# One exponential per pair of heads over two adjacent PSUM banks, and waits per K-chunk for the first output tile of three projections, in an eight-core hybrid (state space, attention, gated FFN) kernel

## The reference, cut to what matters

```python
g = y * silu(z)
g = g * rsqrt(mean(g ** 2) + EPS) * norm_w
x = x + einsum('bld,df->blf', g, out_proj_w)      # state-space layer, its end
...
r = sigmoid(xr @ W_r.T);  k = xk @ W_k.T          # FFN
x = x + r * (square(relu(k)) @ W_v.T)
...
att = einsum('bhqd,bhkd->bhqk', q, k) * (1.0 / sqrt(D))      # attention, 16 heads
att = softmax(where(causal, att, -inf), axis=-1)
x = x + einsum('bhqk,bhkd->bhqd', att, v) @ w_proj + b_proj
```

## Time and profile before

| | |
|---|---|
| median of 2 runs | 9809.84 us (9798.19 to 9821.5) |
| the profiled execution | 9709.57 us |
| its span, slowest core (5) | 9708.0 us (all cores 9662.8 to 9708.0) |
| TensorE matmuls, weight loads | 5080.3 us (52%), 2045.3 us (21%) |
| VectorE | 3306.1 us (34%) |
| ScalarE | 2614.5 us (27%) |
| mean granted clock of TensorE, core 5 | 0.694 |
| attention, all blocks, with what lies between them | about 5990 to 8700 us of the span |

### The profile page before, as it was taken

How to read it: one execution, slowest core, us unless ns; L and a number is a source line. 1 busy time by engine, 2 the same in 40 slices (tenths; PEclk the granted TensorE clock), 3 DMA queues, 4 the chain that set the end, 5 groups by cost and what they waited for, 6 DMA issues and landing times.

```text
span 9708.0 us, 88191 instructions; the slowest of 8 cores (9662.8 to 9708.0 us)
## 1 busy us (share of the span) xinstructions
PE 5080.3 (52%) x21232; PEld 2045.3 (21%) x21232; DVE 3306.1 (34%) x6508; ACT 2614.5 (27%) x4592; POOL 148.4 (2%) x234
## 2 busy tenths in 40 slices
PE   0235645646546552555245665566666666653555
PEld 0223223223223230221011221111111111111222
DVE  0444454454444443455323233221110101013444
ACT  0113123122232130000101112355557575741111
POOL 2000000000000000000100000000000000000000
PEclk9556756757657665777567776567778787876776
DMA  6330101101101102000332221100000000002001
GB/s 102 94 102 26 60 9 51 60 1 60 50 10 60 36 24 44 35 35 35 75 82 74 77 65 58 35 28 31 31 19 13 31 1 31 1 18 52 35 37 42
DMA packets 336322, 420.16 MB, mean 43 GB/s; under 512 B 120993, under 2 KB 181026, under 8 KB 335778
## 3 DMA queue, kind: packets, MB, share of 16 engines
q1 hardware_dynamic: 247314, 360.00, 11.8%
q0 software_dynamic: 88528, 54.52, 3.6%
HBM read 331.39 MB, written 119.87 MB: 46 GB/s over the span
## 4 chain that ended last, share of the span: by engine, by line
PE 36%; DVE 23%; ACT 16%; DMA 11%; issue 11%; DVEq 1%; SPq 1%; POOL 1%; ACTq 1%; POOLq 0%
ACT pt_sb L191 10%; PE pB L191 9%; PE pA L191 7%; PE pE L191 6%; PE pD L191 5%; PE pF L191 4%; PE pC L191 4%; ACT D L191 3%; DVE y L191 2%; DVE t1b L191 2%; DMA wtmp<-win_l 2%; DVEq L189 1%; DMA xtm<-x 1%; ACT tr L191 1%; DMA wq_sb<-wqkv_l 1%
## 5 line engine op out<-in xcount | busy, mean ns | idle before, releaser
L191 DVE TENSOR_TENSOR pt_sb<-pt_sb,mask01b 128x128 bf16<-128x128 bf16 x512 | 115.4, 225 | 1865.0 <-ACT pt_sb L191 1864.0
L191 PE MATMUL pB<-pt_sb,vb 128*65 128x512 bf16 (+3 forms) x1152 | 498.7, 433 | 368.1 <-ACT pt_sb L191 300.3
L191 ACT ACTIVATE pt_sb<-pE,ebias 128x512 bf16<-128x512 f32 x576 | 382.3, 664 | 892.4 <-PE pE L191 811.6
L191 PE MATMUL pA<-pt_sb,vb 128*65 128x512 bf16 (+3 forms) x1152 | 508.0, 441 | 128.7 <-DVE pt_sb L191 29.3
L191 PE MATMUL pA<-r_t,wr_sb 128*128 128x512 bf16 x512 | 146.4, 438 | 633.6 <-DVE h L191 633.6
L191 ACT ACTIVATE pt_sb<-pF,ebias 128x512 bf16<-128x512 f32 x576 | 382.2, 664 | 90.3 <-PE pD L191 3.9
L191 PE MATMUL pE<-qq_sb,K_sb 64*128 64x512 bf16 x576 | 259.2, 450 | 258.0 <-DVE den_t L191 189.4
L191 ACT ACTIVATE pt_sb<-pC,ebias 128x512 bf16<-128x512 f32 (+1 forms) x576 | 368.6, 640 | 85.5 <-PE pD L191 0.4
L191 ACT ACTIVATE pt_sb<-pD,ebias 128x512 bf16<-128x512 f32 (+1 forms) x576 | 368.7, 640 | 85.2
L191 ACT ACTIVATE sig_t<-pA 128x512 bf16<-128x512 f32 x64 | 38.2, 597 | 1146.7 <-PE pA L191 1146.6
L191 DVE TENSOR_TENSOR Gm<-E,Gmsk 128x1024 bf16<-128x1024 f32 x128 | 156.9, 1226 | 556.3 <-ACT E L191 556.3
(11 more groups left out here) (293 smaller groups left out, 9325.8 us busy)
## 6 DMA issues: line engine op xcount, KB each, us to landing
winm<-winb_h SPq DMA_DIRECT2D x272, 256.0 KB, 2.6
wq_sb<-wqkvb_h SPq DMA_DIRECT2D x192, 256.0 KB, 2.6
xrtB<-xres SPq DMA_DIRECT2D x16, 2048.0 KB, 8.6
xrtC<-xres SPq DMA_DIRECT2D x16, 2048.0 KB, 11.2
xtm<-x SPq DMA_DIRECT2D x32, 512.0 KB, 4.4
xres<-xcs SPq DMA_DIRECT2D x32, 512.0 KB, 3.2
xrt<-xres SPq DMA_DIRECT2D x8, 2048.0 KB, 13.5
xres<-xrt SPq DMA_DIRECT2D x8, 2048.0 KB, 6.9
```

The costliest lines, as they stand in the source:

```text
L191: ins = getattr(h, ent[1])(*ent[2], **ent[3])
```

## The change

PSUM banks C and D become the two halves of one tensor `pCD`, and E and F those of `pEF`, with the old names as views. In the attention both score matmuls of a step are issued first and one mark is taken behind the second. Where the tile has 512 or 384 columns (`off <= 128`), one ScalarE instruction then takes the exponential of both banks, 1024 or 896 columns, into two adjacent slots of `pt_sb`; with 384 columns it also covers the 128 unused columns of the first slot, which nothing reads. For 256 and 128 columns there are two instructions as before, the first of which carries all the waits. Both banks are free after the later one, and both V products wait for their exponential's mark (for a merged one that is the same mark). The masks of VectorE then follow both exponentials. In the three projections the matmuls of the first output tile each wait for their own chunk's mark; the other tiles wait for the last one as before.

```diff
@@ -277,8 +277,13 @@
         setattr(c, nm, al(nm, sh, dt).ap())
 
     c.pbank = {}
-    for nm in ["A", "B", "C", "D", "E", "F"]:
+    for nm in ["A", "B"]:
         c.pbank[nm] = nc.alloc_psum_tensor("p" + nm, [128, 512], F32).ap()
+    for pnm in ["CD", "EF"]:
+        pp = nc.alloc_psum_tensor("p" + pnm, [128, 1024], F32).ap()
+        c.pbank[pnm] = pp
+        c.pbank[pnm[0]] = pp[:, 0:512]
+        c.pbank[pnm[1]] = pp[:, 512:1024]
     c.pbank["T1"] = nc.alloc_psum_tensor("pT1", [128, 1024], BF16).ap()
     c.pbank["T2"] = nc.alloc_psum_tensor("pT2", [128, 1024], BF16).ap()
 
...
@@ -913,12 +918,16 @@
         w_res = {}
         for mo in range(NCH):
             bk = "ABEF"[mo % 4]
-            w = bgw(c, bk) + [w_gn[15], ld_xr]
+            w0 = bgw(c, bk) + [ld_xr]
             for kc in range(16):
+                if mo == 0:
+                    w = (w0 if kc == 0 else []) + [w_gn[kc]]
+                else:
+                    w = (w0 + [w_gn[15]]) if kc == 0 else []
                 S.op("tensor", "matmul", pb[bk][:, 0:512],
                      c.woutb[:, kc * 1024 + mo * 128:kc * 1024 + (mo + 1) * 128],
                      y2[:, kc * 512:(kc + 1) * 512],
-                     start=(kc == 0), stop=(kc == 15), waits=w if kc == 0 else [])
+                     start=(kc == 0), stop=(kc == 15), waits=w)
             w_mm = S.ms("tensor")
             if mo == NCH - 1:
                 w_zgate = w_mm
...
@@ -1114,12 +1123,16 @@
         w_res = {}
         for mo in range(NCH):
             bk = "CD"[mo % 2]
-            w = bgw(c, bk) + [w_ka[NCH - 1]]
+            w0 = bgw(c, bk)
             for kc in range(NCH):
+                if mo == 0:
+                    w = (w0 if kc == 0 else []) + [w_ka[kc]]
+                else:
+                    w = (w0 + [w_ka[NCH - 1]]) if kc == 0 else []
                 S.op("tensor", "matmul", pb[bk][:, 0:512],
                      wv_sb[:, kc * 1024 + mo * 128:kc * 1024 + (mo + 1) * 128],
                      kact[:, kc * 512:(kc + 1) * 512],
-                     start=(kc == 0), stop=(kc == 7), waits=w if kc == 0 else [])
+                     start=(kc == 0), stop=(kc == 7), waits=w)
             w_vmm = S.ms("tensor")
             w_vlast = w_vmm
             osl = o_t[:, (mo % 2) * 512:(mo % 2) * 512 + 512]
...
@@ -1430,9 +1443,10 @@
                 if kt < nkt:
                     off = max(0, (kt - 4 * qm) * 128)
                     N = 512 - off
+                    s0 = 2 * (kt % 2)
+                    pair = "EF" if kt % 2 == 0 else "CD"
                     for half in range(2):
-                        h = h0 + half
-                        bks = ("E", "F", "C", "D")[2 * (kt % 2) + half]
+                        bks = ("E", "F", "C", "D")[s0 + half]
                         rows = slice(half * 64, half * 64 + 64)
                         w = bgw(c, bks)
                         if cc == 0 and kt == 0 and qm == 0:
...
@@ -1444,15 +1458,31 @@
                              qq_sb[rows, cc * 512 + off:(cc + 1) * 512],
                              start=True, stop=True,
                              tile_position=(half * 64, 0), waits=w)
-                        w_s = S.ms("tensor")
-                        psl = pt_sb[:, (2 * (kt % 2) + half) * 512:
-                                    (2 * (kt % 2) + half) * 512 + N]
-                        w = [w_s] + ([w_pv_slot[(kt % 2, half)]]
-                                     if (kt % 2, half) in w_pv_slot else [])
-                        S.op("scalar", "activation", psl, pb[bks][:, 0:N], AF.Exp,
-                             bias=c.ebias[:, 1:2], scale=0.125, waits=w)
-                        w_e = S.ms("scalar")
-                        bgs(c, bks, w_e)
+                    w_s = S.ms("tensor")
+                    wl = [w_s]
+                    for half in range(2):
+                        if (kt % 2, half) in w_pv_slot:
+                            wl.append(w_pv_slot[(kt % 2, half)])
+                    if off <= 128:
+                        S.op("scalar", "activation",
+                             pt_sb[:, s0 * 512:s0 * 512 + 512 + N],
+                             pb[pair][:, 0:512 + N], AF.Exp,
+                             bias=c.ebias[:, 1:2], scale=0.125, waits=wl)
+                        w_es = [S.ms("scalar")] * 2
+                    else:
+                        w_es = []
+                        for half in range(2):
+                            S.op("scalar", "activation",
+                                 pt_sb[:, (s0 + half) * 512:(s0 + half) * 512 + N],
+                                 pb[pair][:, half * 512:half * 512 + N], AF.Exp,
+                                 bias=c.ebias[:, 1:2], scale=0.125,
+                                 waits=wl if half == 0 else [])
+                            w_es.append(S.ms("scalar"))
+                    bgs(c, pair[0], w_es[1])
+                    bgs(c, pair[1], w_es[1])
+                    for half in range(2):
+                        psl = pt_sb[:, (s0 + half) * 512:(s0 + half) * 512 + N]
+                        w_e = w_es[half]
                         if kt >= 4 * qm:
                             S.op("vector", "tensor_mul", psl[:, 0:128], psl[:, 0:128],
                                  c.mask01b, waits=[w_e])
...
@@ -1531,12 +1561,16 @@
             w = [w_wp_used[gm2 - 3]] if gm2 >= 3 else []
             ld_w = S.dma("sync", wsl, wpb_h[mo], waits=w, ch="cw%d" % b)
             bk = ("E", "F", "C", "D")[mo % 4]
-            w = bgw(c, bk) + [ld_w, w_norm[NCH - 1], ld_xr]
+            w0 = bgw(c, bk) + [ld_w, ld_xr]
             for kc in range(NCH):
+                if mo == 0:
+                    w = (w0 if kc == 0 else []) + [w_norm[kc]]
+                else:
+                    w = (w0 + [w_norm[NCH - 1]]) if kc == 0 else []
                 S.op("tensor", "matmul", pb[bk][:, 0:512],
                      wsl[:, kc * 128:(kc + 1) * 128],
                      yraw[:, kc * 512:(kc + 1) * 512],
-                     start=(kc == 0), stop=False, waits=w if kc == 0 else [])
+                     start=(kc == 0), stop=False, waits=w)
             S.op("tensor", "matmul", pb[bk][:, 0:512],
                  bprojb[0:1, mo * 128:(mo + 1) * 128], ones512,
                  start=False, stop=True)
```

## The result

The changed kernel takes 9421.77 us (median of 11 runs, 9320.19 to 9475.75) against 9794.12 us (10 runs, 9691.99 to 9835.01) for the kernel before: a ratio of 0.9614, 95% interval 0.9565 to 0.9664. The forecast was 9454 us and a saving of 356 us, or 0.963. It is faster, by 372 us.

What follows compares the result with a forecast made beforehand. ScalarE's exponentials were taken to bound the attention step at either clock level. Savings of 261 + 23 + 22 + 26 + 24 = 356 us, off the median 9809.8, gave 9454 us (ratio 0.963), range 9340 to 9560 us.

Steps and rivals of the forecast that it cites:

- The exponential of 1024 columns: Attention off the diagonal: merged exponential takes 1.114 us, a higher-clock step 1.262 in place of 1.670 us, ScalarE still the bound.
- 640 steps at the higher clock: Attention: 640 of the steps off the diagonal run at 2.4 GHz and save 0.408 us each, 261 us.
- The lower clock: Attention at 1.2 GHz: TensorE becomes the bound at 1.51 us a step, 0.16 less, 266 steps, 43 us.
- The pair's start and its end: Head pairs: start loses 0.35 us in 56 pairs, 20 us; diagonal end gains 0.35 us in 64, 22 us.
- State space: Output projection: first tile's matmuls run between VectorE's chunks, 3.24 us a block, 26 us; clock not raised in advance.
- FFN: Value projection: seven matmuls fit into the 1.97 us wait for `kact`, 1.51 us a block, 24 us over 16 blocks.
- Attention's projection: First matmul still needs the weight's DMA, so 0 us saved, 3 us at most.
- TensorE's ring: Attention: products, next scores and return to ScalarE take 1.16 us after an exponential, 0.25 us inside the 1.41 available.
- only the gap goes: Rival, attention: one instruction over two banks costs as much as two; saving 190 us, 9620 us; chance 0.08.
- the clock stays low: Rival, attention: new rhythm holds TensorE at 1.2 GHz, all 896 steps 1.51 us; 195 us saved, 9615 us; chance 0.05.
- all weight loads hide: Rival, attention: lower-clock steps also take 1.26 us, 65 us more saved, 9389 us; chance 0.04.
- the overlap is lost: Rival, attention: scores, exponential and products follow in a ring, 2.27 us a step; slower, 10300 us; chance 0.03.

Runs made afterwards that it cites:

- experiment 4: Kernel before, nothing merged, with the four slots of `pt_sb` as four tensors, so most self-waits of exponentials go: 9354.7 us, ratio 0.9592.
- experiment 2: Kernel before with only the three projections' waits per chunk, banks and exponentials as before: 9753.92 us, ratio 1.0002.
- experiment 3: Changed kernel with the pair never merged, two exponentials of 512 columns under the new shared marks: 9690.2 us, ratio 0.9932.
- experiment 11: Unmerged kernel before with four slot tensors, early scores and chunk waits, and no self-wait of any exponential: 9067.3 us, ratio 0.9344.
- experiment 12: Changed kernel with two slot tensors, early scores, strided diagonal exponentials, and no self-wait of any exponential: 9139.59 us, ratio 0.9402.
- experiment 9: Kernel before, unmerged, with four slot tensors, early scores and the projections' chunk waits: 9188.77 us, ratio 0.9417.
- experiment 5: Changed kernel with the two pairs of slots of `pt_sb` as two tensors: 9299.29 us, ratio 0.9537.
- experiment 8: Changed kernel with two slot tensors, the late wait for A and B, and all pairs merged: 9176.89 us, ratio 0.9417.
- experiment 10: Kernel of experiment 8 once more, on the same chip as experiment 9: 9191.51 us, ratio 0.9388.
- experiment 1: Changed kernel with the three projections' waits put back as before, merged exponentials kept: 9444.03 us, ratio 0.9693.
- experiment 6: Changed kernel with the wait for A and B moved from a pair's first scores to its first V products: 9271.03 us, ratio 0.9517.
- experiment 7: Changed kernel with all pairs merged, the diagonal ones by a strided pattern over both banks: 9332.7 us, ratio 0.9591.

## Why the prediction was right

The forecast of 0.963 lies inside the measured interval, and the mechanism is the one given. By its steps:

- *The exponential of 1024 columns* takes 1.113 us, worked out 1.114; the step at the higher clock is 1.263 us on average, worked out 1.262. ScalarE stayed the bound. The hidden load between A and B was assumed and is there (0.21 us, and 0.43 at the lower clock).
- *640 steps at the higher clock* is the term that was mis-sized. The count was right for the kernel before: core 5, whose rows the forecast used, has 639, and the cores 639 to 665. That it would stay was assumed. The changed kernel has 707 of 896 on core 5 and 704 to 711 over the cores. In the kernel before 17 to 44 lower-clock steps by core lay in the middle of a pair, behind steps at the higher clock; in the changed kernel there is none on any core. The lower-clock steps with which a pair begins also became fewer, from 207 to 214 a core to 185 to 192. In these runs the granted clock didn't fall inside a pair where TensorE's matmuls stood closer: experiment 4, with as many ScalarE instructions as before and a step of 1.29 us, has no such step either, and experiments 2 and 3, with 1.67 and 1.62 us, keep 19 to 46 and 12 to 33 by core. On core 0 the 896 steps, the last one of each pair among them, took 1.693 us on average before, at either level. In the changed kernel the 706 at the higher level take 1.292 us, which gives 283 us, 22 more than forecast.
- *The lower clock* was forecast at 43 us before the pair's start. The 190 that are left on core 0 take 1.510 us on average, 0.18 less than before, which gives 35.
- *The pair's start and its end*, -20 and +22 us, made +2; the turn measured from the first diagonal product to the next pair's first went from 9.90 to 9.68 us, which is 14 us over 64 pairs. How much of it belongs to either was not taken apart; the diagonal's products show that the clock had a part in it, with 363 ns for those of 384 columns (above) against 472 in the same group of the kernel before on core 0. With these 14 in place of 2, the parts add up to 332 us against the 333 measured over the periods.
- *State space* 26 us forecast, 26 measured, and the clock was not raised ahead of time, as assumed.
- *FFN* 24 us forecast, some 14 + 7 measured. The first FFN gives its 12 and a little more. In the second one TensorE's clock gives part back. Its groups before (core 7) and after (core 2), the receptance and key projections that lead up to the value projection:

```profile
L191 PE MATMUL pA<-r_t,wr_sb 128*128 128x512 bf16 x256 | 73.1, 437 | 316.6 <-DVE h L191 316.6
L191 PE MATMUL pB<-ka_t,wk_sb 128*128 128x512 bf16 x256 | 63.1, 391 | 0.0
```

```profile
L191 PE MATMUL pA<-r_t,wr_sb 128*128 128x512 bf16 x256 | 73.6, 440 | 316.5 <-DVE h L191 316.5
L191 PE MATMUL pB<-ka_t,wk_sb 128*128 128x512 bf16 x256 | 66.9, 409 | 0.0
```

  They are busy 4.3 us longer with the same work, which is about what is missing. Why their clock rises later there and not in the first FFN stays open.
- *Attention's projection* 0 forecast; the DMA is the wait, and nothing was gained that the rows show.

So the total is right to 16 us, with the attention 27 us too small, for the most part by the count of higher-clock steps, and the FFN 3 us too large. The parts exceed the medians' difference by 8 us, and no run tells where they are. That the saving comes so close is in part luck, since the misses of its terms, +22, +12, -8 and -3 us, and those 8 us partly cancel. The time itself was forecast 32 us too high, 16 by the saving and 16 by the base. Of the rivals, *only the gap goes* fell with the 1.113 us; *the clock stays low* with 706 steps at the higher level; *all weight loads hide* with 1.53 us at the lower one; *the overlap is lost* with the step of 1.26, although both V products do wait for the whole exponential.

What the prediction had right in size it had not understood in kind. It booked the step's 0.408 us as 0.262 for a second instruction's fixed part and 0.148 for the gap. Experiments 4 and 11 show that without the self-wait two exponentials of 512 columns start 0.57 us apart, not 0.835: the self-wait costs 0.265 us each time, the gap of 0.148 and 0.12 of lost overlap. So 0.265 of the 0.408 us are one self-wait less, and only the rest, 0.14, is what a second instruction costs. And where TensorE's ring holds the step, that rest gives less still: 1.160 us unmerged (11) against 1.135 merged (12). With the waits gone merging brings nothing that the sums show, 1561 us against 1542 unmerged.

## What to carry to other kernels

When an engine waits for its own last instruction, look for the gap that the timeline puts no releaser to, and ask whether the wait is needed before making the instructions fewer: here a slot's reader already ordered its writes, and with the wait taken away the unmerged kernel's attention took no longer than the merged one's (1542 against 1561 us, all else alike). Follow a recorder's automatic waits in the order of the program, since giving each slot its own name moved the wait to every fourth instruction and did not remove it. And where TensorE's matmuls are moved closer, count the steps at each clock level anew: the level itself moves.

## What the runs showed that was not expected

- Exponentials back to back overlap. 512 columns take 0.687 us by their record, yet start 0.57 us apart when none waits for the one before, and 1024 columns, 1.11 us, start 1.01 us apart (for 512 columns experiments 4, 9 and 11, for 1024 experiments 5, 8, 10 and 12). The Trainium skill, "ScalarE: Activation LUTs", section "What ACT_TABLE_LOAD costs", states an overlap of about 93 ns for back-to-back activations; the runs agree in kind, with 117 ns for 512 columns and 100 for 1024. The prediction drew on this section for the length of an exponential and left the overlap out: with no exponential of the kernel before overlapping another, no row of it showed that the self-wait had a second price. The records hide it. The groups by form of experiment 11 give 742 ns for each, more than in the kernels before it, while the starts lie 570 ns apart:

```profile
L191 ACT ACTIVATE pt_sb<-pE,ebias 128x512 bf16<-128x512 f32 x512 | 380.1, 742 | 713.0 <-PE pE L191 602.6 <-PE pF L191 109.9
```

  What a stream of them costs is read from the starts.
- A self-wait that stands alone on an instruction costs less than one beside a wait for another engine: 0.78 us from start to start in experiment 3 (1.47 - 0.69) against 0.835.
- The drops of the clock inside a head pair, 17 to 44 steps a core, are absent on all cores of every kernel whose step at the higher clock was 1.29 us or less (experiments 1, 4 to 12), and present in those with a step of 1.62 or more (2 and 3). No kernel lies between, so the runs set no limit.
- Between V products and scores the weight load stays exposed in the changed kernel too: 0.31 us from one to the other at the higher clock and 0.53 to 0.57 at the lower, while A to B takes 0.21 and 0.43.
